# A fused attention and feed-forward kernel: the residual's scaling moved into the first twisted key round, finer waits before three stages, one sum of the second pair of heads moved ahead

## The reference, cut to what matters

```python
x = x + _L0_xattn_ref(_layernorm(x), ctx_4096, mask, bias, ln_weight, w_q, w_k, w_v, w_out)

def _L0_xattn_ref(hidden_states, key_value_states, attention_mask, position_bias, ...):
    x = _rmsnorm(hidden_states, ln_weight)
    h_q = (x @ w_q.T).reshape(b, lq, 32, 128)
    h_k = (key_value_states @ w_k.T).reshape(b, lk, 32, 128)
    h_v = (key_value_states @ w_v.T).reshape(b, lk, 32, 128)
    score = einsum('bqhd,bkhd->bhqk', h_q, h_k) + position_bias
    score = softmax(where(mask, score, -inf))
    attn = einsum('bhqk,bkhd->bqhd', score, h_v)
    return hidden_states + attn @ w_out.T
```

## Time and profile before

| | us |
|---|---|
| median of 3 executions | 1614.78 |
| lowest and highest | 1614.23, 1615.2 |
| the profiled execution | 1615.26 |
| its span, first to last instruction | 1613.5 |
| PE busy in it | 1598.8 |

### The profile page before, as it was taken

The page is one execution under the profiler, slowest core; times in us unless marked ns, Lnnn a source line. Parts: engine busy times, 40 slices in busy tenths (PEclk is TensorE's granted clock), DMA queues, the critical chain, the costliest instruction groups (busy, mean ns, idle before and its releaser), DMA issues.

```text
span 1613.5 us, 25021 instructions
## 1 busy us (share of the span) xinstructions
PE 1598.8 (99%) x8512; PEld 1365.9 (85%) x8512; DVE 999.5 (62%) x1528; ACT 748.1 (46%) x1922; POOL 878.4 (54%) x688
## 2 busy tenths in 40 slices
PE   9989999999999999999999999999999999999999
PEld 7878888888888888888888887888898898889887
DVE  7523333636666676676679677776656656665675
ACT  5331111225454544554553334656645546654653
POOL 6344444537466575565569775544536435443445
PEclk9999999999999999999999999999999999999999
DMA  9434444513333332333341211101100111010011
GB/s 345 172 125 157 153 151 153 180 40 130 108 120 106 107 123 94 107 123 94 114 150 47 59 41 50 60 33 33 53 34 27 47 40 33 27 47 20 21 53 53
DMA packets 52111, 146.44 MB, mean 91 GB/s; under 512 B 7264, under 2 KB 12000, under 8 KB 51520
## 3 DMA queue, kind: packets, MB, share of 16 engines
q1 hardware_dynamic: 52032, 145.41, 26.0%
HBM read 107.64 MB, written 37.75 MB: 90 GB/s over the span
## 4 chain that ended last, share of the span: by engine, by line
PE 94%; DVE 2%; POOL 1%; ACT 1%; issue 1%; DMA 0%; SPq 0%; ACTq 0%; DVEq 0%; POOLq 0%
PE banks L55 27%; PE banks L57 26%; PE banks L56 26%; PE banks L2283 4%; PE banks L783 3%; PE banks L803 3%; PE banks L792 2%; PE banks L2290 2%; PE banks L224 1%; ACT resid L993 0%; DMA rawA<-in_x_wK 0%; DVE resid L1933 0%; POOL wtA_lo L1428 0%; ACT x_probs L1055 0%; DMA g_swapped<-in_l_b 0%
## 5 line engine op out<-in xcount | busy, mean ns | idle before, releaser
L2747 POOL TENSOR_TENSOR g_swapped<-g_swapped,rawB 128x512 f32<-128x512 f32 x80 | 103.0, 1290 | 171.2 <-ACT g_swapped L2429 171.2
L1526 POOL TENSOR_TENSOR x_probs<-x_probs,x_inv 128x512 f32<-128x512 f32 x64 | 66.6, 1040 | 170.9 <-DVE x_inv L1317 168.0
L1055 ACT ACTIVATE x_probs<-x_probs,x_top 128x128 f32<-128x128 f32 x256 | 99.5, 390 | 92.2 <-DVE x_top L1308 92.2
L1428 POOL TENSOR_TENSOR wtA_lo<-rawA,wtA_hi 128x1024 fp32r<-128x1024 f32 (+1 forms) x31 | 72.1, 2326 | 100.2 <-ACT wtB_hi L964 78.8
L1193 DVE COPY c_v_kept<-banks 128x512 f32<-128x512 f32 x64 | 44.1, 690 | 108.1 <-PE banks L57 108.1
L2577 DVE TENSOR_TENSOR g_turned_by<-banks,rawB 128x512 f32<-128x512 f32 x80 | 55.2, 690 | 85.8 <-ACT g_swapped L2429 85.8
L2741 POOL TENSOR_TENSOR g_probs<-g_probs,g_inv 128x512 f32<-128x512 f32 x64 | 67.7, 1079 | 74.5 <-DVE g_inv L2568 74.4
L55 PE MATMUL banks<-wtV_hi,g_att_lo 128*128 128x512 f32 x256 | 104.3, 407 | 0.0
L55 PE MATMUL banks<-xT_hi,wtO_lo 128*128 128x512 f32 x256 | 102.9, 402 | 0.0
L2428 ACT COPY g_swapped<-banks 64x512 f32<-64x512 f32 x80 | 46.7, 583 | 120.3 <-PE banks L57 113.6
L56 PE MATMUL banks<-wtV_lo,g_att_hi 128*128 128x512 f32 x256 | 100.3, 392 | 0.0
(11 more groups left out here) (353 smaller groups left out, 5155.2 us busy)
## 6 DMA issues: line engine op xcount, KB each, us to landing
kept_k<-c_k_kept SPq DMA_DIRECT2D x16, 1024.0 KB, 4.0
x_k<-kept_k SPq DMA_DIRECT2D x32, 512.0 KB, 4.5
kept_v<-c_v_kept SPq DMA_DIRECT2D x14, 1024.0 KB, 4.9
x_v<-kept_v SPq DMA_DIRECT2D x28, 512.0 KB, 3.5
rawA<-in_x_wQ SPq DMA_DIRECT2D x16, 512.0 KB, 4.4
rawO<-in_x_wO SPq DMA_DIRECT2D x16, 512.0 KB, 3.5
rawO<-in_g_wQ SPq DMA_DIRECT2D x16, 512.0 KB, 3.5
rawV<-in_g_wO SPq DMA_DIRECT2D x16, 512.0 KB, 3.5
```

The costliest lines, as they stand in the source:

```text
L1055: e = nc.scalar.activation(probs[:, b, :], probs[:, b, :], ACT.Exp, bias=top[:, b:b + 1], accum_out=total[:, b:b + 1])
L1428: return pool.tensor_tensor(wt[into][1][:, cut], raw[kind][:, cut], f32(wt[into][0][:, cut]), ALU.subtract)
L1526: pool.tensor_tensor(probs[:, part, :], probs[:, part, :], rows, ALU.mult).then_inc(probs_ready, 1)
L2747: pool.tensor_tensor(part, part, sin[:, :].unsqueeze(1).to_broadcast([P, HB, P]), ALU.mult)\
```

## The change

Five edits, all in the first attention.

- PE, first step of `seven_keys`: the one wait for `vo_added` of 8 becomes three, 5 + X = 5 ahead of the product into X, 5 + Y = 6 (and the wait for the twisted context) ahead of Y, 5 + Z = 7 ahead of Z.
- ACT: the eight `add_hidden` go from the end of round 1 to places in round 1 behind the first `key_weights`: one, `high(5)`, three, `high(6)`, three, `high(7)`, one. POOL's `twice_of` goes from the end of round 1 to the end of round 0.
- PE, last outputs: the wait for `att_lo` of 64 becomes one for 63 ahead of sequence 0 and one for 64 ahead of sequence 4 (behind the first head's part of sequence 4).
- ACT: `output_weights(0)`, the cast of the first output weights, goes from the end of the first pair into pair 1, behind both `attn_hi` and `first_copy`.
- DVE: `inverse(1, 1)` goes from the end of the first pair into pair 1, behind the first sum; `two_sums` is cut into `first_sum` and `next_sums` for that.

```diff
@@ -677,13 +677,18 @@
                 n = key_step(i, which)
                 weights_ready("A", 2 + n + 1)
                 pe.wait_ge(qk_copied, 8 + 2 * n)
-                if isinstance(i, int) and i == 1 and which == 0:
-                    pe.wait_ge(vo_added, 8)
-                    key_twist.ready(pe, 4)
+                first = isinstance(i, int) and i == 1 and which == 0
+                if first:
+                    pe.wait_ge(vo_added, 5 + X)
                 else:
                     pe.wait_ge(q_sums, 5 * n)
                 part(X, a11, c11)
+                if first:
+                    key_twist.ready(pe, 4)
+                    pe.wait_ge(vo_added, 5 + Y)
                 part(Y, s2, ct2)
+                if first:
+                    pe.wait_ge(vo_added, 5 + Z)
                 part(Z, s1, ct1)
                 pe.wait_ge(qk_copied, 8 + 2 * n + 1)
                 part(X, a12, c21, True)
@@ -901,10 +906,11 @@
             first_head(2)
             pv(LAST, 1, 1)
             first_head(3)
-            pe.wait_ge(att_lo, 4 * PAIRS)
             for b in range(B):
                 if b >= HB:
                     first_head(b)
+                if b % HB == 0:
+                    pe.wait_ge(att_lo, 4 * PAIRS - 1 + b // HB)
                 output_part(LAST, b, 1, LAST_O).then_inc(vo_made, 1)
                 if b >= 4:
                     norm.turn(pe, b - 4)
@@ -1036,17 +1042,21 @@
                     high(4)
                 key_weights(key_step(i, 0) + 1)
                 if second:
-                    for b in range(5, B):
-                        high(b)
+                    add_hidden(0)
+                    high(5)
+                    for b in range(1, 4):
+                        add_hidden(b)
+                    high(6)
+                    for b in range(4, 7):
+                        add_hidden(b)
+                    high(7)
+                    add_hidden(7)
                 key_copy(i, 1)
                 key_quarter(i, 1)
                 if isinstance(i, int) and i == QUADS - 2:
                     last_key_weights()
                 else:
                     key_weights(key_step(i, 1) + 1)
-                if second:
-                    for b in range(B):
-                        add_hidden(b)
 
             def exps(n, j):
                 act.wait_ge(top_ready, 2 * n + j + 1)
@@ -1107,7 +1117,6 @@
                 probs_turned(0, 1)
                 exps(1, 0)
                 exps(1, 1)
-                output_weights(0)
 
             def body(g, last):
                 a, b_ = 2 * g, 2 * g - 1
@@ -1116,6 +1125,8 @@
                 attn_hi(a - 2, 0, 0)
                 first_copy(g)
                 attn_hi(a - 2, 1, 0)
+                if isinstance(g, int) and g == 1:
+                    output_weights(0)
                 first_quarter(g)
                 probs_turned(b_, 0)
                 probs_turned(b_, 1)
@@ -1332,12 +1343,14 @@
 
             s00, s01, s10, s11 = (q[:, h, token_half(j)] for h in range(2) for j in range(2))
 
-            def two_sums(g):
+            def first_sum(g):
                 dve.wait_ge(qk_copied, K_COPIED + 2 * g + 1)
                 if not isinstance(g, int) or g:
                     dve.wait_ge(scores_ready, 4 * g)
                 dve.wait_ge(qk_made, K_UNITS + 7 * g + 2)
                 query_sum(s01, Y, s10)
+
+            def next_sums(g):
                 dve.wait_ge(qk_made, K_UNITS + 7 * g + 5)
                 query_sum(s11, Y, s10)
                 dve.wait_ge(q_sums, K_SUMS + 5 * g + 2)
@@ -1358,7 +1371,8 @@
                 value(0)
                 value(1)
                 value(2)
-                two_sums(0)
+                first_sum(0)
+                next_sums(0)
                 value(3)
                 logits(0, 0)
                 fourth_sum(0)
@@ -1373,13 +1387,15 @@
                 logits(1, 0)
                 logits(1, 1)
                 inverse(1, 0)
-                inverse(1, 1)
 
             def body(g, last):
                 a, b_ = 2 * g, 2 * g - 1
                 attn_lo(a - 2, 0, 0)
                 attn_lo(a - 2, 1, 0)
-                two_sums(g)
+                first_sum(g)
+                if isinstance(g, int) and g == 1:
+                    inverse(1, 1)
+                next_sums(g)
                 logits(a, 0)
                 fourth_sum(g)
                 fifth_sum(g)
@@ -1468,6 +1484,7 @@
                     pool.wait_ge(power_set, 2)
                     scale_of(0)
                     scale_of(1)
+                    twice_of()
                     return
                 value_weights(i)
                 for which in range(2):
@@ -1479,7 +1496,6 @@
                         combine(n, n + 2, ("A", n + 2))
                         seven_low(n + 3)
                 if isinstance(i, int) and i == 1:
-                    twice_of()
                     mask_of()
                 if isinstance(i, int) and i == QUADS - 2:
                     value_weights(QUADS - 1)
```

## The result

The changed kernel takes 1605.24 us in the median (1605.11 to 1605.78, 4 executions) against 1614.62 beside it; the ratio is 0.9943 with a 95% interval of 0.9928 to 0.9958. Timed again in five rounds it was 1605.71 against 1614.68, 0.9942 (0.9929 to 0.9956). So it is 9.4 and 9.0 us faster. The forecast was 1604.9, 9.9 faster, with a range of 1603.7 to 1607.4.

The account below looks back on a forecast made before the run. PE, busy 1598.8 of 1613.5 us, was taken to bound the kernel. The terms 7.07 + 0.80 + 1.06 + 0.98 = 9.91 us came off 1614.78, giving 1604.9, with a range of 1603.7 to 1607.4.

Parts of the forecast that it names:

- Round 2: Start of the second round: PE's wait for ACT's key copy and the slow matmuls behind it both go, 7.07 us.
- two reserves taken from round 3: Time to spare before PE needs ACT's key copy, 1.32 us, and POOL's low value weights, 0.62, assumed for the second round.
- Where the work went: Round 1 on ACT and POOL's idle time before 53.80: the moved residual operations and factor cost nothing.
- Bank waits: Start of round 1: PE no longer waits for all eight value copies before its first twisted key step, 0.80 us.
- Pair 1: Start of the second attention pair: the first query sum comes in time for PE, 1.06 us gained.
- The doubt about the small product: Moved inverse: if DVE's 4-element product again took 2.12 us, all of the 1.06 us gain would go.
- Last outputs: End of the first attention: PE starts without waiting for the second half of attn_lo, 0.98 us gained.
- the first: Rounds or second pair: another wait replaces a removed one; about 1606, down to 1607.4 with two; chance 0.17.
- the third: Second round: PE still stands there because another wait was covered; only 2.84 us come, 1611.9; chance 0.05.
- the fourth: Loops over pairs: passes wait for their instructions and the kernel gets slower, 1619.3 at 1.2 us a pass; chance 0.03.
- The second: Second round: the clock stays low for a while, so 2.71 us are not returned, 1607.6; chance 0.05.

Follow-up runs that it names:

- the exchange on POOL: Changed kernel with the second inverse of head 1 back at the first pair's end and POOL's normalisation ahead of its bias in pair 1: 1605.46 us.

## Why the prediction was right, and where its size was off

- **Round 2.** The mechanism held: the chain from POOL's factor through ACT's operations to the key copy is shown by putting both back (6.73 us return) and by moving the factor alone (all of it goes). The two reserves taken from round 3 held to the digit: 1.32 for the copy, and the 0.62 of POOL was met when ACT was delayed by 1 us. **The size was off here.** The 7.07 was the loss of one execution. Priced by starts the wait is 4.36 to 4.38 in each, but the slow stretch behind it cost 2.71 in the trace that I read, 1.71 and 1.72 in two others of the same kernel (9.26 - 3.17 - 4.38 and 9.25 - 3.17 - 4.36), and 2.36 with the edits undone. The prediction named 4.36 and 7.07 as bounds and took the upper one; the term should have stayed between them, since the slow stretch was a single event in a single profile. The forecast gain still came within 0.5 and 0.9 us of the two measured ones, since this error is at most 1 us in a sum of 9.9.
- **Where the work went.** Costless, as said. The gap for the last operation ahead of the second key copy was 0.86 and it took 0.82; the copy started at 76.56. POOL's five instructions ran in idle time. The prediction treated the spreading as what lets the operations be hidden; one run shows that it was not needed.
- **Bank waits.** 0.80 forecast, 0.79 and 0.80 by the table and by undoing.
- **Pair 1.** 1.06 forecast, 1.03 to 1.05 found. The doubt about the small product was the right one to raise, and the exchange on POOL settled it: it is slow only where it starts beside a POOL instruction. Of the Trainium skill's rule ("SBUF — State Buffer", SBUF: two separate sides) these rows bear out that the product waits. That every POOL instruction reading SBUF holds the port for its whole length they do not: on DVE two centrings of the input, with more than one SBUF input, took 1.41 us (0.74 each, as one alone) while POOL raised eight numbers per partition to a power in 1.67 us. Beside POOL's weight split the same centring took 2.89. Timelines of POOL and DVE:

```profile
40.59 1.67 POOL L1463 TENSOR_TENSOR rstd<-var_eps,power 128x8 f32<-128x8 f32 x1
40.91 1.41 DVE L1191 SCALAR_TENSOR_TENSOR s_centred<-resid,moments,row 128x512 f32<-128x512 f32 x2
...
53.47 2.42 POOL L1444 TENSOR_TENSOR wtV_lo<-rawV,wtV_hi 128x1024 fp32r<-128x1024 f32 x1 [10.26 <-ACT wtV_hi L921]
53.54 2.89 DVE L1191 SCALAR_TENSOR_TENSOR s_centred<-resid,moments,row 128x512 f32<-128x512 f32 x1
```

So the prediction's fear that the moved factor could hold up the centring by up to 1.67 us did not come true. Why the power lets DVE through and the split does not stays open.

- **Last outputs.** 0.98 forecast, 0.96 to 0.98 found; the wait for the normalised input stayed (0.52).
- **The sum.** With 6.08 in place of 7.07 for round 2, from the third trace of the kernel before, the four terms are 6.08 + 0.79 + 1.04 + 0.96 = 8.87; with the first trace they are 9.9. The medians stood 9.38 and 8.97 apart, between the two. Most of the remaining scatter is at the start, where the third product began anywhere from 8.33 to 9.53 in the traces of this study.
- **Rivals.** None of the four came: the table of waits has no new one, against the first and the third, and the time is 9.4 us lower, against the fourth. (PE gained three waits by the edits, ahead of Y, of Z and of sequence 4, and not the two that the prediction counts.) The second, that the clock stays low without the wait, is contradicted by a granted clock of 1.00 there and by the slow stretch that copies on ACT alone brought about.

## What to carry to other kernels

Price a wait by the starts on both sides of it, not by its idle time, and read the slow matmuls behind it as an amount that changes from execution to execution. Before moving work that stands on the critical path, ask what it waited for: here one small chain of five instructions on another engine was the whole of 6 to 7 us. And take the reserve for the new order from another pass of the same loop; it told both what would hold and which wait comes next.

## What the runs showed of the hardware that I had not expected

- After the same wait of 4.2 us the matmuls ran at half pace for eight to twelve starts, in different executions of the same kernel, so 1.7 to 2.7 us were lost beside the wait.
- A wait of 1.97 us was enough for a slow stretch, in the one execution that had it, and it began some 1.5 us behind the wait, with PE busy again; the waits of 0.5 to 0.9 us that I looked at had none.
- A DVE product of 4 elements per partition took 2.12 us beside a POOL instruction and 0.16 without it. DVE's centring of 512 elements took 2.89 us beside POOL's weight split and 0.74 while POOL raised eight numbers per partition to a power.
